# Layer 0's finish with gate and output matmuls as 64-row tiles, one column parity in each half of TensorE's array

## The chip, the cores and the metric

The kernel runs on one core of a Trainium2 chip. Its engines work side by side, each through its own instructions in order: TensorE (PE in the profile, and PEld for its weight loads) multiplies matrices into the accumulation memory PSUM, VectorE (DVE) and ScalarE (ACT) read PSUM and work elementwise, GpSimd (POOL) works elementwise on SBUF, SyncE (SP) issues the transfers. They wait for each other by semaphores. PSUM has 128 partitions and eight banks of 512 f32 columns. The metric is the device time of one execution in microseconds; lower is better.

## The reference

x is a 256 x 256 grid of tokens of 64 channels. Two layers follow each other, each added to x. What the change touches is the end of layer 0, the "finish": from the products p and from zn (the normalised input of the layer) it makes the output.

```python
p = jnp.einsum('bikc,bjkc->bijc', a, b)
x = _ln(p, ln_out_w, ln_out_b) @ w_z + b_z
g = jax.nn.sigmoid(zn @ w_g + b_g)
return x * g                       # and outside: x = x + this
```

## The kernel before

One partition row of the kernel's tiles holds two neighbouring tokens of 64 channels, an even and an odd column of the grid. So weights of 64 x 64 stand twice in a 128 x 128 matrix whose two other quarters are zero: `w_out` (in EFF) for the output and columns E_G to E_Z of `w_hi` and `w_lo` (EFF read as f16) for the gate. 128 partitions in, 128 columns out: partitions and columns 0 to 63 are the even tokens, 64 to 127 the odd ones.

Layer 0's finish goes over NG = 64 groups of GR = 4 grid rows, in 67 steps of a software pipeline that is written out by hand for each engine; nothing but these orders and the semaphores decides when something runs. In step s TensorE does, in this order:

- four transposes of the normalised p of group s (`pn` in WK, f32, line 752), when DVE and POOL have each written their half of it (pn_done, pn_done_p);
- the gate of group s (`project_gate`, line 486 through `mm`, tiles EFF and XT_ALL), for s >= AHEAD = 4: 12 matmuls of 128 x 128 in f16, three products for each of four rows. The gates of groups 0 to 3 are made ahead, at the end of the chunk loop. Gate g goes to PSUM bank g % 2, and waits until the sigmoid of group g-2 has read that bank (sg_done at g-1);
- the output z of group s-1 (line 486): the bias in one matmul of 512 columns (BROW, ONES), then four f32 matmuls of 128 x 128, each of which is two weight loads and two passes on the chip (EFF, WK). The transposed data `pt` is the stationary operand, w_out the moving one. z goes to bank 6 + (s-1) % 2 and waits until DVE has read group s-3 out of it (y_done);
- four transposes of the new x of group s-3 (f32, line 784).

ACT copies the transposed p to `pt` (line 964), takes the gate's sigmoid out of PSUM into `sg` (line 969), and splits off the high f16 part of the new x (line 977). DVE normalises half of pn (line 1420), multiplies z out of PSUM by sg, which is called y here (line 1429), makes the low f16 part of the new x (line 1443) and its statistics (line 1435). POOL normalises the other half of pn (line 1030) and adds y to x (line 1039). In DVE's steps 3, 6 and 9 a chain of four instructions (`rstd_rows`, lines 1365 to 1368) stands between pn and y; it makes the next quarter of the reciprocal deviations. Transfers of p and x run under all this.

In the chunk loop of both layers `project` already has units in two forms: with 128 rows, and, where `split_rows` says so, with 64-row matmuls whose two halves of the array work on the two column halves and write to two banks.

Of the kernel before, what the change touches and what calls it, by code (L numbers as in the profile page):

```python
# [34 lines left out]
CH = 64  # L35
P = 128
ROW = 2 * CH
GR = 4
# [13 lines left out]
AHEAD = 4  # L52
# [14 lines left out]
E_G = NQ * 2 * QW  # L67
# [21 lines left out]
def build(nc, x, mask, w0, w1, bias0, bias1, vecs, consts, norm_consts, spread, ones3, out):  # L89
# [4 lines left out]
    ALU = mybir.AluOpType  # L94
    ACT = mybir.ActivationFunctionType
# [10 lines left out]
    with ctx:  # L106
# [14 lines left out]
        BROW = sb("BROW", ROW, bf16)  # L121
        ONES3 = sb("ONES3", P, bf16)
# [7 lines left out]
        T = sb("T", 36)  # L130
        table_tmp = sb("table_tmp", 12)
        PS = ctx.enter_context(nc.psum_tensor("PS", [P, 8, BANK], f32))


        w_hi, w_lo = (EFF[:, 0:E_Z].bitcast(f16)[:, i * E_Z:(i + 1) * E_Z] for i in range(2))

        def half(g, i):

            return halves[:, ds(g * (2 * BANK) + i * BANK, BANK)]
# [71 lines left out]
        pt = WK[:, 6 * BANK:8 * BANK].rearrange("p (s n) -> p s n", s=2)  # L211
# [75 lines left out]
        g_done = sem("g_done")  # L287
        sg_done = sem("sg_done")
# [49 lines left out]
        def mask_tile(eng, n4, u):  # L338
# [2 lines left out]
            return eng.tensor_tensor(ab[:, :, :, ds(n4 * (4 * PR) + u * PR, PR)], sig[:, u],  # L341
                                     rows.unsqueeze(2).to_broadcast([P, 2, 2 * CHUNK, PR]), ALU.mult)

        def reached(eng, semaphore, value):

            if not isinstance(value, int) or value > 0:
                eng.wait_ge(semaphore, value)
# [136 lines left out]
        def _(pe):  # L484
            def mm(dst, lhsT, rhs, start=True, stop=True):
                return nc.tensor.matmul(dst, lhsT, rhs, start=start, stop=stop)  # L486
# [100 lines left out]
            for layer in range(2):  # L587
# [3 lines left out]
                def rows_times(bank, g, r, column):  # L591

                    dst = bank[:, r * ROW:(r + 1) * ROW]
                    hi, lo = (half(g, i)[:, r * P:(r + 1) * P] for i in range(2))
                    mm(dst, hi, w_hi[:, ds(column, ROW)], True, False)
                    mm(dst, hi, w_lo[:, ds(column, ROW)], False, False)
                    return mm(dst, lo, w_hi[:, ds(column, ROW)], False, True)
# [39 lines left out]
                        last.then_inc(proj_done[layer], 1)  # L637

                def project_gate(g):
                    if layer == 0:  # L640
                        for r in range(GR):
                            last = rows_times(PS[:, g if g < AHEAD else g % 2, :], g, r, E_G)
                        last.then_inc(g_done, 1)
                    else:
                        bank, hi, lo = PS[:, g % 4, :], w_hi[:, E_G:E_Z], w_lo[:, E_G:E_Z]
                        mm(bank, hi, half(g, 0), True, False)
                        mm(bank, lo, half(g, 0), False, False)
                        mm(bank, hi, half(g, 1), False, True).then_inc(gate1_done, 1)
# [96 lines left out]
                for step in range(NG + 3):  # L745
                    g = step
                    if g < NG:
                        pe.wait_ge(pn_done, g + 1)
                        pe.wait_ge(pn_done_p, g + 1)
                        reached(pe, pt_ready, g - 1)  # L750
                        for r in range(GR):
                            last = nc.tensor.transpose(PS[:, 4 + g % 2, r * P:(r + 1) * P], pn[:, g % 2, r, :], ident)  # L752
                        last.then_inc(tb_done, 1)
                    if AHEAD <= g < NG:

                        pe.wait_ge(sg_done, g - 1)
                        project_gate(g)
                    g = step - 1
                    if 0 <= g < NG:

                        pe.wait_ge(pt_ready, g + 1)
                        reached(pe, y_done, g - 1)
                        bank = PS[:, 6 + g % 2, :]
                        mm(bank, ONES3[:, :], BROW[:, :].unsqueeze(1).to_broadcast([P, GR, ROW]), True, False)
                        for r in range(GR):
                            last = mm(bank[:, r * P:(r + 1) * P], pt[:, g % 2, r * P:(r + 1) * P], w_out,
                                      False, r == GR - 1)
                        last.then_inc(z_done, 1)
                    g = step - 3
                    if 0 <= g < NG:  # L770

                        pe.wait_ge(xadd_done, g + 1)
                        if g < 2:

                            pe.wait_ge(sg_done, g + 3)
                        if g < NG - 2:

                            reached(pe, x1split_done, g - 1)
                        else:

                            pe.wait_ge(sg_done, NG)
                        for r in range(GR):
                            row = g * GR + r
                            last = nc.tensor.transpose(PS[:, new_x_bank(g), r * P:(r + 1) * P],  # L784
                                                       xb[:, row // HR % HS, row % HR, :], ident)
                        last.then_inc(x1tr_done, 1)
# [13 lines left out]
        def _(act):  # L800
# [55 lines left out]
            for layer in range(2):  # L856
# [99 lines left out]
                def finish_steps(g0, n_steps, lo):  # L956

                    for k in range(n_steps):
                        g = g0 + k
                        if lo[0] <= k < lo[1]:  # L960
                            act.wait_ge(tb_done, g + 1)

                            reached(act, z_done, g - 1)
                            nc.scalar.activation(pt[:, k % 2], PS[:, 4 + k % 2, :], ACT.Copy).then_inc(pt_ready, 1)
                            ahead = isinstance(g, int) and g < AHEAD
                            act.wait_ge(g_done, g + 1)

                            reached(act, xadd_done, g - 3)
                            nc.scalar.activation(sg[k % 4], PS[:, k if ahead else k % 2, :], ACT.Sigmoid,
                                                 scale=T[:, 22:23]).then_inc(sg_done, 1)  # L970
                        if lo[2] <= k < lo[3]:
                            h = g - 4

                            act.wait_ge(x1tr_done, h + 1)
                            act.wait_ge(bn_done, h + (1 + NG))
                            bank = new_x_bank(h) if isinstance(h, int) else 2 + k % 2
                            nc.scalar.activation(half(h, 0), PS[:, bank, :], ACT.Identity, scale=T[:, 25:26]
                                                 ).then_inc(x1t_ready, 1)
# [100 lines left out]
        def _(dve):  # L1079
# [228 lines left out]
            for layer in range(2):  # L1308
# [95 lines left out]
                def finish_steps(g0, n_steps, lo):  # L1404

                    for k in range(n_steps):
                        g = g0 + k
                        if lo[0] <= k < lo[1]:
                            s, u = (k // BG) % 2, k % BG
                            if u == 0:  # L1410

                                dve.wait_ge(p_in[s], g0 * 4 + 64)

                            reached(dve, tb_done, g - 1)

                            src = ptb[:, s].rearrange("p (c q) (r e) -> p q c r e", q=2, e=2)
                            dst = pn[:, k % 2].rearrange("p r (q c e) -> p q c r e", q=2, e=2)
                            tile = src[:, 0, :, u * GR:(u + 1) * GR, :]
                            rs = rstd2[:, 0, ds(g * GR, GR)].unsqueeze(1).unsqueeze(3)
                            ins = V.tensor_tensor(dst[:, 0], tile, rs.to_broadcast([P, CH // 2, GR, 2]), ALU.mult)  # L1420
                            ins.then_inc(pn_done, 1)
                            if isinstance(g0, int) and g0 == 0 and k in (3, 6, 9):
                                final(rstd_rows(k // 3), rstd_ready, k // 3)
                        if lo[2] <= k < lo[3]:
                            h = g - 2
                            dve.wait_ge(z_done, h + 1)
                            dve.wait_ge(sg_done, h + 1)
                            tile = sg[(k + 2) % 4]
                            V.tensor_tensor(tile, PS[:, 6 + k % 2, :], tile, ALU.mult).then_inc(y_done, 1)
                        split(k, g, lo)  # L1430
                        if lo[4] <= k < lo[5]:
                            h = g - 4
                            dve.wait_ge(x1tr_done, h + 1)
                            bank = new_x_bank(h) if isinstance(h, int) else 2 + k % 2
                            V.bn_stats(REC[:, ds(h * 6, 6)], PS[:, bank, :]).then_inc(bn_done, 1)
# [146 lines left out]
```

## Time and profile before

| what | us |
|---|---|
| median of three runs (lowest, highest) | 1107.92 (1107.46, 1108.34) |
| the profiled execution: its own time | 1107.85 |
| the profiled execution: span from first to last instruction | 1105.8 |
| TensorE busy, of the span | 997.5 (90%) |
| VectorE busy | 804.0 (73%) |
| ScalarE busy | 681.7 (62%) |
| GpSimd busy | 556.9 (50%) |

Busy times of an engine are summed over the whole program, whose stages have different limits. TensorE's matmuls overlap in its pipeline and their ends are modelled, so the distance from start to start says more of its pace than a busy share. The finish lies between 507 and 683 us of the span.

### The profile page before, as it was taken

What the parts mean: (1) busy time and instruction counts of PE and PEld (TensorE: products, weight loads), DVE (VectorE), ACT (ScalarE), POOL (GpSimd) and SP (SyncE); (2) the same over time, 40 slices, a digit from 0 to 9 for tenths busy, and PEclk for the clock granted to TensorE, in tenths of its full rate; (3) what the DMA queues carried; (4) which work ended last, traced back from release to release, by engine and by line L of the source; (5) the groups of instructions that cost most, each with busy time, mean ns of one, the idle gap of its engine ahead of it and who ended that gap; (6) DMA issues with size and microseconds to landing.
All of it is one profiled execution on the core that took longest, in us unless ns stands there. A gap on an engine that the chain in (4) does not pass through costs nothing.

```text
span 1105.8 us, 36355 instructions
## 1 busy us (share of the span) xinstructions
PE 997.5 (90%) x14204; PEld 780.1 (71%) x14204; DVE 804.0 (73%) x1270; ACT 681.7 (62%) x1102; POOL 556.9 (50%) x479
## 2 busy tenths in 40 slices
PE   5689798579999999996999997799999999789997
PEld 5543333248898888985999997587878787645554
DVE  6926988976786868767988888664646565567775
ACT  5747565365666656655676765484857667546665
POOL 0000644488092561904777774390937648146664
PEclk9989999869999999998999998799999999989999
DMA  9800000000301203069999760004031130599994
GB/s 349 317 9 1 0 1 0 1 2 4 134 24 78 78 22 134 4 181 231 226 208 203 180 149 1 2 4 154 5 104 54 46 111 4 167 196 285 294 276 153
DMA packets 173196, 121.32 MB, mean 110 GB/s; under 512 B 69764, under 2 KB 152068, under 8 KB 173064
## 3 DMA queue, kind: packets, MB, share of 16 engines
q1 hardware_dynamic: 173064, 119.34, 39.9%
q8 instruction: 110, 1.80, 0.7%
q14 instruction: 22, 0.18, 0.1%
HBM read 68.99 MB, written 50.33 MB: 108 GB/s over the span
## 4 chain that ended last, share of the span: by engine, by line
PE 77%; DVE 9%; DMA 4%; issue 4%; POOL 3%; ACT 2%; SPq 1%; DVEq 0%; POOLq 0%; ACTq 0%
PE PS L486 69%; DMA AB<-x 3%; PE PS L737 3%; PE PS L752 2%; PE PS L784 2%; DVE AB L1259 1%; POOL XT_ALL L994 1%; POOL AB L341 1%; DVE XT_ALL L1280 1%; DMA AB<-k_scratch 1%; PE PS L500 1%; DVE XT_ALL L1443 1%; ACT WK L874 1%; SPq L355 0%; DVE WK L1316 0%
## 5 line engine op out<-in xcount | busy, mean ns | idle before, releaser
L486 PE MATMUL PS<-EFF,XT_ALL 64*128 64x64 f16 (+1 forms) x10368 | 342.6, 201 | 8.7 <-POOL XT_ALL L994 3.6
L486 PEld LDWEIGHTS PS<-EFF,XT_ALL 64*128 64x128 f16 (+1 forms) x10368 | 315.5, 96 | 42.7 <-issue 16.9
L486 PE MATMUL PS<-AB 128*128 128x256 f16 (+3 forms) x1482 | 291.5, 348 | 36.3 <-ACT AB L841 10.6
L486 PEld LDWEIGHTS PS<-AB 128*128 128x128 f16 (+3 forms) x1482 | 200.9, 137 | 124.6 <-issue 34.0
L874 ACT ACTIVATE WK<-PS,T 128x512 f32<-128x512 f32 x256 | 174.7, 685 | 94.9 <-PE PS L486 82.8
L1059 POOL TENSOR_TENSOR AB<-WK,AB 128x512 f32 x128 | 144.8, 1162 | 111.8 <-ACT AB L884 110.8
L341 POOL TENSOR_TENSOR AB<-WK,MS 128x512 f32 x96 | 130.5, 1389 | 104.5 <-DVE WK L1316 104.5
L994 POOL TENSOR_TENSOR XT_ALL<-AB,XT_ALL 128x512 f32 (+1 forms) x59 | 69.8, 1192 | 166.5 <-DVE XT_ALL L1280 156.2
L1069 POOL TENSOR_TENSOR WK<-XT_ALL 128x512 f32 (+1 forms) x64 | 82.0, 1283 | 76.5 <-PE PS L737 51.1
L1324 DVE TENSOR_TENSOR WK<-PS,WK 128x512 f32<-128x512 f32 x128 | 85.8, 686 | 33.2 <-ACT WK L874 33.2
L1316 DVE TENSOR_TENSOR WK<-PS,WK 128x512 f32<-128x512 f32 x128 | 86.8, 688 | 30.1 <-ACT WK L874 23.4
L1340 DVE BATCH_NORM_STATS2 REC<-WK 128x512 f32 x64 | 44.4, 694 | 56.9 <-ACT WK L903 56.9
L925 ACT ACTIVATE WK<-PS,T 128x512 f32<-128x512 f32 x64 | 49.4, 777 | 51.5 <-PE PS L486 51.5
L836 ACT ACTIVATE XT_ALL<-PS,T,CF 128x512 f32<-128x512 f32 (+1 forms) x64 | 49.7, 776 | 49.6 <-PE PS L486 49.6
L903 ACT ACTIVATE WK<-PS,T 128x512 f32<-128x512 f32 x64 | 44.0, 687 | 51.8 <-PE PS L486 51.8
L910 ACT ACTIVATE WK<-PS 128x512 f32<-128x512 f32 x64 | 41.2, 644 | 47.0 <-PE PS L486 47.0
L486 PE MATMUL PS<-AB,EFF 128*128 128x512 f32 x128 | 67.5, 613 | 2.4 <-DMA AB<-k_scratch 2.4
L486 PEld LDWEIGHTS PS<-EFF,WK 128*128 128x128 f32 x512 | 68.1, 194 | 1.8
L486 PE MATMUL PS<-XT_ALL,AB 128*128 128x512 f32 (+1 forms) x128 | 68.8, 626 | 0.0
L1030 POOL TENSOR_TENSOR WK<-AB,S 128x256 f32<-128x256 f32 x64 | 50.7, 792 | 36.0 <-DVE S L1368 35.4
L486 PE MATMUL PS<-EFF,WK 128*128 128x128 f32 x512 | 68.3, 277 | 0.0
L1335 DVE TENSOR_TENSOR S<-S,WK 128x512 f32<-128x512 f32 x64 | 44.5, 695 | 31.9 <-ACT WK L910 30.9
(193 smaller groups left out, 1537.4 us busy)
## 6 DMA issues: line engine op xcount, KB each, us to landing
AB<-x SPq DMA_DIRECT2D x64, 512.0 KB, 7.0
p_scratch<-WK SPq DMA_DIRECT2D x32, 512.0 KB, 2.6
k_scratch<-WK SPq DMA_DIRECT2D x64, 256.0 KB, 2.1
AB<-k_scratch SPq DMA_DIRECT2D x32, 512.0 KB, 10.4
out<-AB SPq DMA_DIRECT2D x16, 1024.0 KB, 8.6
AB<-p_scratch SPq DMA_DIRECT2D x29, 512.0 KB, 7.6
AB<-p_scratch SPq DMA_DIRECT2D x2, 640.0 KB, 6.3
RAW<-w SPq DMA_DIRECT2D x2, 256.0 KB, 2.7
```

The source lines that it names most:

```text
L341: return eng.tensor_tensor(ab[:, :, :, ds(n4 * (4 * PR) + u * PR, PR)], sig[:, u], rows.unsqueeze(2).to_broadcast([P, 2, 2 * CHUNK, PR]), ...
L486: return nc.tensor.matmul(dst, lhsT, rhs, start=start, stop=stop)
L836: nc.scalar.activation(XT[:, ds(n * GR, GR), :].rearrange("p r n -> p (r n)"), PS[:, u % 4, :], ACT.Identity, bias=T[:, 15:16], scale=CF[: ...
L874: nc.scalar.activation(tile, unit(layer, u)[:, :, 0:2 * CHUNK, :], ACT.Sigmoid, scale=T[:, 22:23] if layer == 0 else T[:, 28:29]).then_inc ...
L925: nc.scalar.activation(gate1[:, k % 4], PS[:, k % 4, :], ACT.Sigmoid, bias=T[:, 32:33], scale=T[:, 28:29]).then_inc(gate1_ready, 1)
L994: nc.gpsimd.tensor_tensor(half(n, 1), zn[:, u % 8], half(n, 0), ALU.subtract).then_inc(lo_done, 1)
L1030: nc.gpsimd.tensor_tensor(dst[:, 1], src[:, 1, :, u * GR:(u + 1) * GR, :], rs.to_broadcast([P, CH // 2, GR, 2]), ALU.mult).then_inc(pn_don ...
L1059: nc.gpsimd.tensor_tensor(ab_rows(ab_lo, n8, u), sig1[:, u], ab_rows(ab_hi, n8, u), ALU.subtract).then_inc(ablo_done, 1)
L1069: nc.gpsimd.tensor_tensor(x1sum[:, k % 4], half(g, 0), half(g, 1), ALU.add).then_inc(x1sum_done, 1)
L1316: V.tensor_tensor(gate, lin, gate, ALU.mult).then_inc(prod_done[0], 1)
L1324: V.tensor_tensor(gate, lin, gate, ALU.mult).then_inc(prod_done[1], 1)
L1335: V.tensor_tensor(S1[:, :], S1[:, :], st[:, s, :, c % 2], ALU.add).then_inc(s1_done, 1)
```

## The change

For groups from AHEAD on, the gate is made by 64-row matmuls: for each of the 12 products one with partitions 0 to 63 and columns 0 to 63 into bank 0, and one with partitions 64 to 127 and columns 64 to 127 into bank 1. The zero quarters are no longer multiplied. Each bank holds 256 columns, so one group fills half of both banks, and all groups use the same two: the gate of group g waits for the sigmoid of group g-1. The output does the same with banks 6 and 7: two bias matmuls of 256 columns with all 128 rows, then for each row two f32 matmuls of 64 rows by 64 columns; z of group g waits for y of group g-1. The sigmoid and y read two banks through a rearranged access pattern; the elements and the results are as many as before.

```diff
+        def by_row(tile):
+            return tile.rearrange("p (r q c) -> p r q c", r=GR, q=2)
+        def by_parity(bank):
+            return PS[:, bank:bank + 2, 0:GR * CH].rearrange("p q (r c) -> p r q c", r=GR)
...
                 def project_gate(g):
-                    if layer == 0:
+                    if layer == 0 and g < AHEAD:
                         for r in range(GR):
-                            last = rows_times(PS[:, g if g < AHEAD else g % 2, :], g, r, E_G)
+                            last = rows_times(PS[:, g, :], g, r, E_G)
+                        last.then_inc(g_done, 1)
+                    elif layer == 0:
+                        for r in range(GR):
+                            hi, lo = (half(g, i)[:, r * P:(r + 1) * P] for i in range(2))
+                            for i, (x, w) in enumerate(((hi, w_hi), (hi, w_lo), (lo, w_hi))):
+                                for q in range(2):
+                                    rows = slice(q * CH, (q + 1) * CH)
+                                    last = mm(PS[:, q, r * CH:(r + 1) * CH], x[rows, :],
+                                              w[rows, E_G + q * CH:E_G + (q + 1) * CH], i == 0, i == 2)
                         last.then_inc(g_done, 1)
...
-                        pe.wait_ge(sg_done, g - 1)
+                        pe.wait_ge(sg_done, g)
...
-                        reached(pe, y_done, g - 1)
-                        bank = PS[:, 6 + g % 2, :]
-                        mm(bank, ONES3[:, :], BROW[:, :].unsqueeze(1).to_broadcast([P, GR, ROW]), True, False)
+                        reached(pe, y_done, g)
+                        for q in range(2):
+                            row = BROW[:, q * CH:(q + 1) * CH].unsqueeze(1).to_broadcast([P, GR, CH])
+                            mm(PS[:, 6 + q, 0:GR * CH], ONES3[:, :], row, True, False)
                         for r in range(GR):
-                            last = mm(bank[:, r * P:(r + 1) * P], pt[:, g % 2, r * P:(r + 1) * P], w_out,
-                                      False, r == GR - 1)
+                            for q in range(2):
+                                rows = slice(q * CH, (q + 1) * CH)
+                                last = mm(PS[:, 6 + q, r * CH:(r + 1) * CH], pt[rows, g % 2, r * P:(r + 1) * P],
+                                          w_out[rows, rows], False, r == GR - 1)
...
+                                nc.scalar.activation(by_row(sg[k % 4]), by_parity(0), ACT.Sigmoid,
+                                                     scale=T[:, 22:23]).then_inc(sg_done, 1)
...
-                            V.tensor_tensor(tile, PS[:, 6 + k % 2, :], tile, ALU.mult).then_inc(y_done, 1)
+                            V.tensor_tensor(by_row(tile), by_parity(6), by_row(tile), ALU.mult).then_inc(y_done, 1)
```

TensorE's program, one step of the finish once all parts run, before (752 the transposes of p, 784 those of x, 486 gate, bias and output; the last two numbers are partitions of the result by columns):

```order
L752 MATMUL PS<-CF,WK 128x128 [waits pt_ready,pn_done_p,pn_done]
L752 MATMUL PS<-CF,WK 128x128 x3
L486 MATMUL PS<-EFF,XT_ALL 128x128 [waits sg_done]
L486 MATMUL PS<-EFF,XT_ALL 128x128 x11
L486 MATMUL PS<-BROW,ONES 128x512 [waits y_done,pt_ready]
L486 MATMUL PS<-EFF,WK 128x128 x4
L784 MATMUL PS<-CF,AB 128x128 [waits x1split_done,xadd_done]
L784 MATMUL PS<-CF,AB 128x128 x3
```

Gate, bias and output follow each other there as 17 calls with 128 rows. The same step in the changed kernel, where the lines have moved to 769, 804 and 494:

```order
L769 MATMUL PS<-CF,WK 128x128 [waits pt_ready,pn_done_p,pn_done]
L769 MATMUL PS<-CF,WK 128x128 x3
L494 MATMUL PS<-EFF,XT_ALL 128x64 [waits sg_done]
L494 MATMUL PS<-EFF,XT_ALL 128x64 x23
L494 MATMUL PS<-BROW,ONES 128x256 [waits y_done,pt_ready]
L494 MATMUL PS<-BROW,ONES 128x256
L494 MATMUL PS<-EFF,WK 128x64 x8
L804 MATMUL PS<-CF,AB 128x128 [waits x1split_done,xadd_done]
L804 MATMUL PS<-CF,AB 128x128 x3
```

The gate has 24 matmuls of 64 columns for 12 of 128, the bias two for one, the output eight for four. The places of the waits in the row order are the same; their values are one group later.

TensorE's program at the start of the finish, the outputs of groups 0, 1 and 2, before:

```order
L486 MATMUL PS<-BROW,ONES 128x512 [waits pt_ready]
L486 MATMUL PS<-EFF,WK 128x128 x4
L752 MATMUL PS<-CF,WK 128x128 [waits pt_ready,pn_done_p,pn_done]
L752 MATMUL PS<-CF,WK 128x128 x3
L486 MATMUL PS<-BROW,ONES 128x512 [waits pt_ready]
L486 MATMUL PS<-EFF,WK 128x128 x4
L752 MATMUL PS<-CF,WK 128x128 [waits pt_ready,pn_done_p,pn_done]
L752 MATMUL PS<-CF,WK 128x128 x3
L486 MATMUL PS<-BROW,ONES 128x512 [waits y_done,pt_ready]
L486 MATMUL PS<-EFF,WK 128x128 x4
```

The first wait for y_done stands at the third output. The same place in the changed kernel, up to the output of group 1:

```order
L494 MATMUL PS<-BROW,ONES 128x256 [waits pt_ready]
L494 MATMUL PS<-BROW,ONES 128x256
L494 MATMUL PS<-EFF,WK 128x64 x8
L769 MATMUL PS<-CF,WK 128x128 [waits pt_ready,pn_done_p,pn_done]
L769 MATMUL PS<-CF,WK 128x128 x3
L494 MATMUL PS<-BROW,ONES 128x256 [waits y_done,pt_ready]
L494 MATMUL PS<-BROW,ONES 128x256
L494 MATMUL PS<-EFF,WK 128x64 x8
```

The wait for y_done has moved one output ahead, to that of group 1.

## Rows read from the trace of the kernel before

**Rows 1.** Busy time by engine in 20 us of the finish: us, engines, PEclk, DMA, GB/s.

```profile
540.00:560.00 20.00, 20.00 (x222) 19.73 (x221) 17.55 (x31) 13.79 (x23) 15.03 (x16) 1.00 1.04 219
```

**Rows 2.** Instructions in order of time, one steady step: start, us, engine, line, operation.

```profile
592.09 0.38 PE L486 MATMUL PS<-BROW,ONES 128*128 128x512 bf16 x1
592.29 0.69 ACT L969 ACTIVATE MS<-PS,T 128x512 f32<-128x512 f32 x1
592.31 1.05 PE L486 MATMUL PS<-EFF,WK 128*128 128x128 f32 x8
...
593.20 0.60 PE L784 MATMUL PS<-CF,AB 128*128 128x128 f32 x4
593.40 0.69 DVE L1429 TENSOR_TENSOR MS<-PS,MS 128x512 f32<-128x512 f32 x1 [0.32 <-PE PS L486]
...
593.64 0.60 PE L752 MATMUL PS<-CF,WK 128*128 128x128 f32 x4
...
594.07 0.83 PE L486 MATMUL PS<-EFF,XT_ALL 128*128 128x128 f16 x12
...
594.74 0.38 PE L486 MATMUL PS<-BROW,ONES 128*128 128x512 bf16 x1
```

**Rows 3.** Waits from 536 to 677 us: waiting, for whom, us, times, longest.

```profile
DVE MS L1429 <- PE PS L486: 8.4, 26, 0.3
```

**Rows 4.** The chain that ended last, from 500 to 705 us: start, us, what.

```profile
535.94 1.78 PE PS L486 x21
...
676.38 1.79 PE PS L486 x21
```

**Rows 5.** A 64-row and a 128-row unit of layer 0's projection: timeline and groups.

```profile
207.68 0.87 PE L486 MATMUL PS<-EFF,XT_ALL 64*128 64x64 f16 x48
...
L486 PE MATMUL PS<-EFF,XT_ALL 64*128 64x64 f16 x48 | 0.9, 190 | 0.0
...
208.48 1.34 PEld L486 LDWEIGHTS PS<-EFF,XT_ALL 128*128 128x128 f16 x24
```

**Rows 6.** Weight loads begun as a 64-row and a 128-row unit starts: us, PEld busy.

```profile
207.67:207.70 0.03, 0.02 (x4) 1.00 0.00 0
...
208.47:208.51 0.04, 0.03 (x2) 1.00 0.00 0
```

**Rows 7.** f32 weight loads outside the finish, in order of time.

```profile
85.43 0.30 PEld L486 LDWEIGHTS PS<-CF,AB 128*128 128x128 f32 x2
85.54 0.28 PE L486 MATMUL PS<-CF,AB 128*128 128x1 f32 x2
85.65 0.30 PEld L486 LDWEIGHTS PS<-XT_ALL,AB 128*128 128x128 f32 x2
...
694.46 0.49 PEld L486 LDWEIGHTS PS<-RAW,EFF 64*128 64x128 f32 x2 [2.95 <-DVE EFF L1474]
...
697.29 0.50 PEld L486 LDWEIGHTS PS<-AB,CF 128*128 128x128 f32 x2 [1.19 <-DVE AB L1134]
```

**Rows 8.** f32 matmuls that change between 128 and 2 rows, in order of time.

```profile
75.28 0.39 PE L486 MATMUL PS<-RAW,AB 128*128 128x128 f32 x2
...
75.60 0.48 PE L486 MATMUL PS<-AB,CF 2*128 2x128 f32 x2
76.01 0.30 PEld L486 LDWEIGHTS PS<-VEC,RAW 128*128 128x128 f32 x2
```

**Rows 9.** The first reciprocal chain of the finish, in order of time.

```profile
514.48 0.38 PE L486 MATMUL PS<-BROW,ONES 128*128 128x512 bf16 x1
...
515.69 0.69 DVE L1429 TENSOR_TENSOR WK<-PS,WK 128x512 f32<-128x512 f32 x1
...
516.77 0.66 PE L752 MATMUL PS<-CF,WK 128*128 128x128 f32 x4 [0.58 <-DVE WK L1420]
```

**Rows 10.** The end of the finish, in order of time.

```profile
678.20 0.69 DVE L1429 TENSOR_TENSOR MS<-PS,MS 128x512 f32<-128x512 f32 x1 [0.69 <-PE PS L486]
...
678.43 0.38 PE L486 MATMUL PS<-BROW,ONES 128*128 128x512 bf16 x1
```

More of the change, by code:

```diff
@@ L968, in finish_steps @@
                             reached(act, xadd_done, g - 3)
-                            nc.scalar.activation(sg[k % 4], PS[:, k if ahead else k % 2, :], ACT.Sigmoid,
-                                                 scale=T[:, 22:23]).then_inc(sg_done, 1)
+                            if ahead:
+                                nc.scalar.activation(sg[k % 4], PS[:, k, :], ACT.Sigmoid,
+                                                     scale=T[:, 22:23]).then_inc(sg_done, 1)
+                            else:
+                                nc.scalar.activation(by_row(sg[k % 4]), by_parity(0), ACT.Sigmoid,
+                                                     scale=T[:, 22:23]).then_inc(sg_done, 1)
                         if lo[2] <= k < lo[3]:
```

## The prediction

> **What bounds the kernel now.** I read the table of busy time by stretch first, to see which engine is full in the finish: in a 20 us piece of it TensorE is busy all the time at a granted clock of 1.00 (2.4 GHz), DVE 17.55 us [rows 1]. Then the timeline of one step, for what TensorE does in it and how fast: from one bias to the next, 592.09 to 594.74, a step takes 2.65 us, and each piece begins where the one before it ends [rows 2]. The waits of this stretch have DVE waiting for TensorE before y (26 times in one of its two forms, 0.3 us at most) and no row with TensorE as the one that waits [rows 3]. The chain that ended last runs through the same TensorE pieces from 535.94 to 676.38, which is 53 steps of 2.65 us [rows 4]. So what the change does to TensorE's step counts in full there, as long as the step stays above DVE's work in it: 17.55 us in 20, so 2.33 us a step.
>
> **The parts of a step before**, from start to start [rows 2]: bias 0.22; output eight passes in 0.89, so 0.111 each; transposes of x 0.44 and of p 0.43, so 0.11 each; gate 12 in 0.67, so 0.056 each. Sum 2.65.
>
> **Gate.** Pairs of 64-row matmuls exist in layer 0's projection. 48 of them take 0.87 us to the end of the last, which is recorded as 0.19 long, so 24 pairs start within 0.68: 0.029 a pair [rows 5]. 24 matmuls of 128 rows take there what they take in the finish (24 loads in 1.34). The gate becomes 12 x 0.029 = 0.35, 0.32 less. The bias keeps its columns, two times 256 for 512: no change but one more short load that lies under the first pass.
>
> **Output.** Here the question is what sets the 0.111 of a pass: its moving columns, which halve, or its weight load, which doesn't. An f32 load shows alone where the matmul has a single column: the loads at 85.43 (two) and 85.65 are 0.22 apart in two, so 0.11 each, though there is next to nothing to stream [rows 7]. So the load already sets the pace, and here the stationary side is pt with 128 columns, before and after. Do 64 rows load faster than 128? At half the clock two loads of 64 rows take 0.49 and two of 128 rows 0.50 [rows 7]: no. The Trainium skill has the same in its page "TensorE: Matmul & The Clock Gate", section "LDWEIGHTS (loading the stationary operand)": the time goes with the columns of the stationary operand and not with its rows. By its formula 128 columns would take an estimated 107 ns, and the trace's f32 loads agree; it speaks against this half of the change.
>
> The eight passes become sixteen with a load each. What remains is whether the loads of the two halves run side by side. At the start of a 64-row unit four loads begin within 0.03 us, two for each half; at the start of a 128-row unit two within 0.04 [rows 6]. The second half's load doesn't wait for the first half's, so I take them as side by side. In program order a row has both passes of the first half, then both of the second. The first half's second pass waits 0.11 for its load, the second half's first pass follows it at once, its second pass 0.11 later. So a row takes 0.225 and four rows, to the end of the last pass (0.055), 0.96 instead of 0.89: 0.07 more. The bounds: were a pair set by its columns alone, 8 x 0.055 = 0.45; were all 16 loads one after another, 16 x 0.111 less the first (which is counted below) plus 0.055 = 1.72. I take 0.96, by the loads' rows.
>
> **Changes of form.** A step now goes 128 rows (transposes), 64 (gate), 128 (bias), 64 (output), 128: four changes where it had none. The last of the 64-row matmuls in [rows 5] starts at 207.68 + 0.87 - 0.19 = 208.36, and the 128-row unit's first load only at 208.48, 0.09 later than the pace would have it. In f32 a pair of 128 rows starts at 75.28 and would be through 0.22 later, at 75.50; the 2-row form's first load stands at 75.60, and the next change comes at 76.01, 0.41 on: two passes (0.22), one bare load (0.11), and again 0.09 of nothing [rows 8]. So a change costs 0.10, both ways, and the load behind it is bare: 0.01 in f16 and bf16, 0.11 in f32. The gate's start and the bias's start cost 0.11 each, the output's start and the transposes' start 0.20 each: 0.62. No wait of another engine covers this, since TensorE is the one that is waited for. The Trainium skill states the cause in "TensorEngine Tiling (Array Packing)", section "Key Properties": changing the tiling mode drains the engine. The trace agrees, with 0.10.
>
> **The step after:** 2.65 - 0.32 + 0.07 + 0.62 = 3.02 us, 0.37 more. 53 steps: 19.6 us.
>
> **The new waits.** In the steady steps they are free. The gate of a group must wait for the sigmoid before it: that starts at 592.29 and takes 0.69, and the next gate starts at 594.07 [rows 2]. z must wait for the y before it: 593.40 + 0.69 = 594.09, the next bias at 594.74 [rows 2], 0.65 to spare; between the last output pass and the next bias lie two sets of transposes, the gate and three changes, over 1.5 us after the change too. ACT's sigmoid and DVE's y read as many elements as before and stay.
>
> At the start they are not free. In step 3 y of group 1 stands on DVE behind the first reciprocal chain and starts at 515.69; z of group 2 started at 514.48, during the chain [rows 9]. It must now wait until 516.38. The first two outputs run at half the clock and push all that by about 0.5. From 516.9 z takes 0.22 + 0.20 + 0.96, then come the change and transposes of x (0.20 + 0.44), and the transposes of p start at 518.9 instead of 516.77 [rows 9]: 2.1 later. Behind them wait gate and z of that step. At the chains of steps 6 and 9 DVE is late anyway and the wait mostly lies under it; four steps between cost 0.37 each, 1.5. Together 3.6, between 1.5 and 6. At the end z of group 63 starts at 678.43, and y of group 62 runs from 678.20 for 0.69 [rows 10]: the wait and the longer output cost about 1.0 in all.
>
> **Sum:** 19.6 + 3.6 + 1.0 = 24.2 us. The profiled execution took 1107.85 (span 1105.8 and 2.05 around it), which is 0.07 below the median of the runs shown, so no correction: 1107.85 + 24.2 = 1132.
>
> **Rivals.** (1) Faster: the halves really halve the output, 0.45 instead of 0.96. The step is 2.51, 0.14 less, 53 of them 7.4, less perhaps 1 us lost at the start: 1101. For it speaks that the f16 pairs halve [rows 5], against it the bare loads of [rows 7]. It decides if an f32 load of 64 rows takes less than about 0.07 us in a running stream, where the step comes out even. The skill's tiling page holds this out in its section "Theoretical Speedup": up to 2 times where the contracted or the moving dimension is 64 or less. By that rule the output would cost 0.45 and the time would be that of this rival; the page gives no trace for f32, and no run here shows it. (2) Slower by much: f32 loads of the two halves share one path and go one after another. The output is 1.72, the step 3.78, 53 x 1.13 = 60, the start 6: 1174. For it speaks only that all rows on loads in pairs are f16, whose loads are short enough to hide an order. (3) No change: the drain costs less here than in the projection, because the transposes of x need no result of the output. The step is even if the four changes and bare loads cost 0.25 instead of 0.62; nothing in [rows 8] speaks for it. Time 1108.
>
> **How the numbers follow.** The mechanism above has 0.79, rival 1 0.09, rival 2 0.08, rival 3 0.04. The likeliest one's own range is 1124 to 1142: steps of 0.30 to 0.45 more (16 to 24 us) with the start between 1.5 and 6 and the end. For 8 in 10 I stretch it to 1116 below and 1150 above, for loads that overlap a little better or worse than in two equal halves; rivals 1 and 2 lie outside. About 0.2% (2 us) is what a measurement of this kernel tells from no change. Faster 0.09, same 0.04, slower 0.87.
>
> **What would show it.** In the profile after: a step from bias to bias of 3.0 us, TensorE still the chain; the gate's 24 matmuls within 0.35 to 0.4; the two weight loads of different halves of the output beginning within a few ns and each 0.11 from the next of its half; 0.1 of nothing at each of four places, and a bare load before the first output pass and the first transpose; DVE waiting longer before y; TensorE waiting for DVE at the first chain. Wrong, if the output's 16 passes take about 0.5 or 1.7 instead of 0.96; if the gaps at the changes are missing; if TensorE waits for the sigmoid or for y in every step; or if the granted clock of the finish falls under the 1.00 it has now.

## The result, and the profile after

The changed kernel takes 1124.14 us (median of four runs, 1122.74 to 1124.86) beside 1108.13 us of the kernel before on the same chip (1107.46 to 1108.82): a ratio of 1.0143, 95% interval 1.0125 to 1.0160. It is slower, by 16 us; the forecast said 24 us, with 1116 to 1150 as its range. The profiled execution spans 1121.9 us, 16.1 more than before.

Where these 16.1 us lie is read from the chain that ended last, 500 to 720 us (start, us, what):

```profile
508.36 1.94 PE PS L769 x8
...
541.84 1.82 PE PS L494 x42
...
692.48 1.84 PE PS L494 x42
700.16 1.89 DVE T L1138
```

The two pieces at 541.84 and 692.48 answer to those of [rows 4] (42 instructions in place of 21: gate 24, bias 2, output 16): 53 steps lie between them, in 150.64 us instead of 140.44, so 2.842 us a step instead of 2.65. That is 10.2 us. From the first transposes, 508.36, to the first of these pieces it takes 33.48 us; before, 508.19 to 535.94, 27.75. That is 5.7 us more at the start. From the last of them to DVE's statistics behind the finish it takes 7.68 instead of 7.18, 0.5 more, and the rest of the program 0.3 less.

One steady step in order of time (start, us, engine, line, operation; PEld are the weight loads), which answers to [rows 2]:

```profile
592.40 0.60 PE L769 MATMUL PS<-CF,WK 128*128 128x128 f32 x4
...
592.94 0.53 PE L494 MATMUL PS<-EFF,XT_ALL 64*128 64x64 f16 x24
...
593.39 0.39 PE L494 MATMUL PS<-BROW,ONES 128*128 128x256 bf16 x2
593.53 0.68 ACT L993 ACTIVATE WK<-PS,T 128x512 f32<-128x512 f32 x1
593.71 0.97 PEld L494 LDWEIGHTS PS<-EFF,WK 64*128 64x128 f32 x16 [0.21 <-issue]
593.72 1.11 PE L494 MATMUL PS<-EFF,WK 64*128 64x64 f32 x16
...
594.75 0.66 PE L804 MATMUL PS<-CF,AB 128*128 128x128 f32 x4
594.87 0.69 DVE L1453 TENSOR_TENSOR MS<-PS,MS 128x512 f32<-128x512 f32 x1 [0.52 <-PE PS L494]
595.14 0.47 PEld L769 LDWEIGHTS PS<-CF,WK 128*128 128x128 f32 x4
595.25 0.60 PE L769 MATMUL PS<-CF,WK 128*128 128x128 f32 x4
```

From start to start: transposes of p 0.54 (before 0.43), gate 0.45 (0.67), bias 0.33 (0.22), output 1.03 (0.89), transposes of x 0.50 (0.44). The gate with the change behind it is 0.22 shorter, everything else is longer. The 16 loads of the output take 0.97 to the end of the last, of which each takes 0.19 (187 ns is the mean of their group from 590 to 600 us): so the last pair begins 0.78 behind the first, which is seven distances of 0.111. That the two halves load side by side shows where the first two begin (loads in a stretch: us, PEld busy):

```profile
593.70:593.73 0.03, 0.02 (x2) 1.00 0.38 102
```

The waits of the finish, 536 to 690 us (waiting, for whom, us, times, longest), beside [rows 3]:

```profile
PEld PS L494 <- issue: 20.5, 108, 0.2
DVE MS L1453 <- PE PS L494: 13.5, 26, 0.5
...
PE PS L494 <- DVE MS L1453: 0.8, 1, 0.8
```

DVE waits 0.5 before y where it waited 0.3, and TensorE itself waits once in the whole stretch, at 539.40, behind the third reciprocal chain: in the steady steps the later values of the two waits cost nothing. The first row is the weight loads' idle time with no releaser, at two places in each step: 0.17 ahead of the gate and 0.21 ahead of the output, two of the four places where the form changes.

### The profile page after: what moved, and what is told of

Read it like the earlier page. It is cut to its first block, busy times and chain, and to the rows that moved or that the text cites. A ratio compares the mean times of both kernels' runs of the same rounds, so it can differ in the third digit from the quotient of the medians.

```text
span 1121.9 us, 38943 instructions
## 1 busy us (share of the span) xinstructions
PE 1012.9 (90%) x15495; PEld 767.8 (68%) x15500; DVE 826.6 (74%) x1270; ACT 675.0 (60%) x1102; POOL 548.4 (49%) x479
## 4 chain that ended last, share of the span: by engine, by line
PE 67%; DVE 12%; issue 9%; DMA 4%; POOL 3%; ACT 2%; DVEq 1%; SPq 1%; POOLq 0%; ACTq 0%; another core or an unknown queue 0%
PE PS L494 61%; DVE WK L1416 4%; PE PS L804 3%; DMA AB<-x 3%; PE PS L769 3%; DVE AB L1283 1%; POOL XT_ALL L1018 1%; POOL AB L341 1%; DVE XT_ALL L1304 1%; DMA AB<-k_scratch 1%; PE PS L508 1%; DVE WK L1420 1%; ACT WK L894 1%; SPq L363 0%; DVE WK L1340 0%
## 5 line engine op out<-in xcount | busy, mean ns | idle before, releaser
L494 PE MATMUL PS<-EFF,XT_ALL 64*128 64x64 f16 (+1 forms) x11088 | 324.8, 198 | 8.7 <-POOL XT_ALL L1018 3.6
L494 PEld LDWEIGHTS PS<-EFF,XT_ALL 64*128 64x128 f16 (+1 forms) x11088 | 295.4, 96 | 52.2 <-issue 26.8
L1093 POOL TENSOR_TENSOR WK<-XT_ALL 128x512 f32 (+1 forms) x64 | 73.8, 1155 | 83.9 <-PE PS L754 58.4
L984 ACT ACTIVATE WK<-PS 128x512 f32<-128x512 f32 x64 | 38.2, 597 | 75.5 <-PE PS L769 75.5
L1420 DVE SCALAR_TENSOR_TENSOR WK<-WK,T 128x512 f32<-128x512 f32 x64 | 76.1, 1189 | 6.7
L494 PEld LDWEIGHTS PS<-EFF,WK 64*128 64x128 f32 x1024 | 65.4, 196 | 14.3 <-issue 14.3
L494 PE MATMUL PS<-EFF,WK 64*128 64x64 f32 x1024 | 74.4, 287 | 0.0
L930 ACT ACTIVATE WK<-PS 128x512 f32<-128x512 f32 x64 | 41.2, 643 | 47.0 <-PE PS L494 47.0
```

What stands on the lines that cost most here:

```text
L1093: nc.gpsimd.tensor_tensor(x1sum[:, k % 4], half(g, 0), half(g, 1), ALU.add).then_inc(x1sum_done, 1)
L1420: V.scalar_tensor_tensor(x1sum[:, k % 4], x1sum[:, k % 4], col(24), gate1[:, k % 4], ALU.mult, ALU.add).then_inc(o_done, 1)
```

## The experiments

The stretch from the first transposes of p to the bias of the tenth output (group 9), read from TensorE's timeline, measures the start below: 28.25 us before (508.19 to 536.44), 33.87 after (508.36 to 542.23).

**The waits alone.** All matmuls have the old form, but the gate has one bank and the output has one, with the changed kernel's waits.

```diff
-                            last = rows_times(PS[:, g if g < AHEAD else g % 2, :], g, r, E_G)
+                            last = rows_times(PS[:, g if g < AHEAD else 0, :], g, r, E_G)
...
-                        pe.wait_ge(sg_done, g - 1)
+                        pe.wait_ge(sg_done, g)
...
-                        reached(pe, y_done, g - 1)
-                        bank = PS[:, 6 + g % 2, :]
+                        reached(pe, y_done, g)
+                        bank = PS[:, 6, :]
...
```

> The kernel before with the single buffering alone: gate and output keep their 128-row form, each on one bank, and wait for the sigmoid and for y of the group just before. Theory A (the 0.19 us that each steady step gained are the form changes of TensorE's array; the new waits cost only at the start of the finish): the steady step stays 2.65 us, only the start gets longer, by 3 to 6 us, so 1111 to 1114. Rival B (the new waits cost in every step): a step near 2.84 and 1120 to 1124.

Measured: 1109.43 us beside 1108.23, ratio 1.0012 (1.0002 to 1.0021). The step is as before, from one bias to the next in TensorE's timeline:

```profile
598.53 0.38 PE L486 MATMUL PS<-BROW,ONES 128*128 128x512 bf16 x1
...
601.18 0.38 PE L486 MATMUL PS<-BROW,ONES 128*128 128x512 bf16 x1
```

2.65 us. The start takes 29.13, 0.9 more. The output of group 2 does wait for y there:

```profile
516.78 0.38 PE L486 MATMUL PS<-BROW,ONES 128*128 128x512 bf16 x1 [1.05 <-DVE WK L1429]
```

It begins 8.33 us after the first transpose, 2.0 later than before the change (514.48 - 508.19 = 6.29). But most of that doesn't last. From 508 us until the tenth output TensorE waits 2.8 us for y in this run, and before the change it waited 2.3 us for DVE at other places of the same steps, ahead of transposes: DVE with its chains is late there either way. So the single buffers cost about 1 us in all, and not the 3.6 that the forecast had for them; most of the changed kernel's 5.7 at the start must have another cause.

**The gate alone** in 64-row matmuls with its wait, bias and output as before:

```diff
-                        reached(pe, y_done, g)
-                        for q in range(2):
-                            row = BROW[:, q * CH:(q + 1) * CH].unsqueeze(1).to_broadcast([P, GR, CH])
-                            mm(PS[:, 6 + q, 0:GR * CH], ONES3[:, :], row, True, False)
+                        reached(pe, y_done, g - 1)
+                        bank = PS[:, 6 + g % 2, :]
+                        mm(bank, ONES3[:, :], BROW[:, :].unsqueeze(1).to_broadcast([P, GR, ROW]), True, False)
...
```

> Only the gate as 64-row matmuls on half of two banks, single buffered; the output as in the kernel before. Theory A: the gate from its first load to the bias takes 0.46 instead of 0.67 and the change of form before it costs 0.09, so a step of 2.53 us, 53 x 0.12 = 6.3 us less, and no lost time at the start since z has its old wait: about 1102. Rival B (waits): the wait for the sigmoid shows in every step, 1108 or more.

Measured: 1102.71 us beside 1108.23, ratio 0.9954 (0.9937 to 0.9971). TensorE's timeline:

```profile
595.29 0.39 PE L494 MATMUL PS<-BROW,ONES 128*128 128x512 bf16 x1
...
597.38 0.53 PE L494 MATMUL PS<-EFF,XT_ALL 64*128 64x64 f16 x24
597.83 0.39 PE L494 MATMUL PS<-BROW,ONES 128*128 128x512 bf16 x1
```

A step of 2.54 us, 0.11 less: 0.32 won by the halves, and two changes of form of 0.10 each paid. The gate's half of the change is a gain.

**The output alone**, the gate as before (gate and sigmoid with two banks, waits one group back):

```diff
-                    elif layer == 0:
...
-                                    last = mm(PS[:, q, r * CH:(r + 1) * CH], x[rows, :],
-                                              w[rows, E_G + q * CH:E_G + (q + 1) * CH], i == 0, i == 2)
...
+                            last = rows_times(PS[:, g if g < AHEAD else g % 2, :], g, r, E_G)
...
```

> Only the output as 64-row matmuls on half of two banks, single buffered, with its two bias matmuls; the gate as in the kernel before. Theory A: bias, output and the transposes of x gain 0.31 us a step (two form changes of 0.1, bare loads, nothing saved in the output's passes): a step of 2.96, 53 x 0.31 = 16.4, and the start's 5.5: about 1130, slower than the whole change. Rival C (64-row passes make the output itself faster, and it is the gate's form that costs): under 1120.

Measured: 1129.60 us, ratio 1.0204 (1.0187 to 1.0222). TensorE's timeline:

```profile
595.38 0.38 PE L494 MATMUL PS<-BROW,ONES 128*128 128x256 bf16 x2
595.69 1.11 PE L494 MATMUL PS<-EFF,WK 64*128 64x64 f32 x16
596.73 0.66 PE L795 MATMUL PS<-CF,AB 128*128 128x128 f32 x4
...
598.33 0.38 PE L494 MATMUL PS<-BROW,ONES 128*128 128x256 bf16 x2
```

A step of 2.95 us, 0.30 more. With the gate's 0.11 less the sum is 0.19 more, which is the changed kernel's step: the two halves of the change add up, and the output's half is the whole loss. Its start takes 32.6 us, so most of the start's loss is the output's too.

**Two changes of form fewer.** The bias is put ahead of the gate, so that gate and output, both in 64-row matmuls, follow each other:

```diff
-                    if AHEAD <= g < NG:
-
-                        pe.wait_ge(sg_done, g)
-                        project_gate(g)
                     g = step - 1
...
                             mm(PS[:, 6 + q, 0:GR * CH], ONES3[:, :], row, True, False)
+                    g = step
+                    if AHEAD <= g < NG:
+
+                        pe.wait_ge(sg_done, g)
+                        project_gate(g)
```

> The changed kernel with one thing moved: in each step the two bias matmuls stand ahead of the gate, so that gate and output follow each other in the 64-row form: two form changes a step instead of four, and the output's first load lies under the gate. The same matmuls, the same bytes. Theory A: 0.09 and 0.10 for the two changes and 0.05 for the bare load fall away: a step of 2.60 us, 53 x 0.24 = 12.8 us less than the changed kernel, about 1111. Rival B (waits): the bias waits for y earlier than before, so no faster than the changed kernel, 1124 or more.

Measured: 1115.05 us, ratio 1.0065 (1.0048 to 1.0082). TensorE's timeline:

```profile
595.14 0.65 PE L807 MATMUL PS<-CF,AB 128*128 128x128 f32 x4
...
596.40 0.52 PE L494 MATMUL PS<-EFF,XT_ALL 64*128 64x64 f16 x24
596.76 1.08 PE L494 MATMUL PS<-EFF,WK 64*128 64x64 f32 x16
597.78 0.66 PE L807 MATMUL PS<-CF,AB 128*128 128x128 f32 x4
```

A step of 2.64 us where the changed kernel has 2.84: two changes fewer save 0.20, so 0.10 each. The expected 2.60 was too low, since I had the output's first load hidden behind the gate; the output still takes 1.02, as its loads only begin when the gate's 24 are through.

**Half the moving columns.** The output passes have 32 columns instead of 64; the second half of each parity's output channels is left out.

```diff
-                                last = mm(PS[:, 6 + q, r * CH:(r + 1) * CH], pt[rows, g % 2, r * P:(r + 1) * P],
-                                          w_out[rows, rows], False, r == GR - 1)
+                                last = mm(PS[:, 6 + q, r * CH:r * CH + CH // 2], pt[rows, g % 2, r * P:(r + 1) * P],
+                                          w_out[rows, q * CH:q * CH + CH // 2], False, r == GR - 1)
```

> The changed kernel with 32 moving columns instead of 64 in each output matmul; the second half of the output channels of each parity is left out. The number of passes and of weight loads stays. Theory A (the output is paced by its f32 weight loads, 0.11 us for each pair): the steady step stays 2.84 us. Rival C (it is paced by its columns): eight pairs by 0.027 less, a step of 2.63.

Measured, in a single run: 1133.29 us beside 1108.41. TensorE's timeline:

```profile
600.62 0.66 PE L804 MATMUL PS<-CF,AB 128*128 128x128 f32 x4
...
602.43 1.08 PE L494 MATMUL PS<-EFF,WK 64*128 64x32 f32 x16
603.44 0.66 PE L804 MATMUL PS<-CF,AB 128*128 128x128 f32 x4
```

The output takes 1.01 instead of 1.03, the step 2.82 instead of 2.84. Half the columns are worth 0.02 us: the loads set the pace of these passes. The time is 9 us longer than the changed kernel's all the same, and that lies at the start (windows: us, engines, PEclk, DMA, GB/s):

```profile
530.00:540.00 10.00, 10.00 (x101) 8.22 (x100) 4.69 (x9) 3.73 (x6) 4.09 (x5) 0.50 0.39 105
...
550.00:560.00 10.00, 10.00 (x180) 8.15 (x178) 7.41 (x14) 5.85 (x10) 6.51 (x7) 0.93 0.41 107
```

The granted clock is 0.50 (1.2 GHz) until 551 us, while TensorE is recorded busy all the time.

**The bias in 64-row matmuls too**, so that gate, bias and output have one form. Its three parts are laid out once, ahead of layer 0, so that each half's rows hold those of its parity:

```diff
-                            row = BROW[:, q * CH:(q + 1) * CH].unsqueeze(1).to_broadcast([P, GR, CH])
-                            mm(PS[:, 6 + q, 0:GR * CH], ONES3[:, :], row, True, False)
+                            rows = slice(q * CH, (q + 1) * CH)
+                            row = BROW[rows, rows].unsqueeze(1).to_broadcast([CH, GR, CH])
+                            mm(PS[:, 6 + q, 0:GR * CH], ONES3[rows, :], row, True, False)
...
```

> The changed kernel with the bias of the output in the 64-row form too: its three bf16 parts stand in rows 0 to 2 and again in rows 64 to 66, and each half of the array makes the bias of its parity. A step has then one stretch of 128 rows (transposes) and one of 64 rows (gate, bias, output). Theory A: two form changes less (0.20, as the run with the bias ahead of the gate showed) and the two bias matmuls side by side (0.11 less): a step of 2.53 us; 53 x 0.31 = 16.4 us less than the changed kernel, the longer start stays: about 1108. Rival: the changes cost only where a load of another type follows, then 2.73 and 1118.

Measured: 1101.50 us beside 1108.41, ratio 0.9936 (0.9920 to 0.9953): faster than the kernel before. TensorE's timeline:

```profile
599.78 0.66 PE L805 MATMUL PS<-CF,AB 128*128 128x128 f32 x4
...
600.80 0.53 PE L494 MATMUL PS<-EFF,XT_ALL 64*128 64x64 f16 x24
601.16 0.27 PE L494 MATMUL PS<-BROW,ONES 64*128 64x256 bf16 x2
601.27 1.00 PE L494 MATMUL PS<-EFF,WK 64*128 64x64 f32 x16
602.21 0.66 PE L805 MATMUL PS<-CF,AB 128*128 128x128 f32 x4
```

A step of 2.43 us (2.45 on average over the 53, as a few are longer). Against the changed kernel the gate saves 0.09 (no change behind it), the bias 0.22 (no change, and its two halves run side by side: 0.11), the output 0.09, because its first loads now begin with the bias, at 601.16. I had expected 2.53, without this last term and with the bias at its old length. DVE has little left to wait now: 19.32 us of 20 are its own work between 540 and 560, so TensorE's step could hardly become shorter with effect.

**The old form at the start.** The outputs of groups 0 to 13 have the old form, banks and wait; all others, and the gates, are the changed kernel's.

```diff
-                        reached(pe, y_done, g)
...
+                        if g < 14:
+                            reached(pe, y_done, g - 1)
+                            bank = PS[:, 6 + g % 2, :]
...
+                                last = mm(bank[:, r * P:(r + 1) * P], pt[:, g % 2, r * P:(r + 1) * P], w_out,
+                                          False, r == GR - 1)
+                        else:
+                            reached(pe, y_done, g)
...
```

> The changed kernel, but the outputs of groups 0 to 13 in the 128-row form on alternating banks, as before the change. Theory D (the 5.6 us lost at the start come from the outputs in their new form there: they keep TensorE at the granted clock of 0.5 until 527 us instead of 513): the clock rises at 512 to 514 us, the tenth output starts 28.2 us after the first transpose of the finish as before the change, later steps take 2.84; with the first steps also shorter, about 1117. Rival E (the single-buffered gate, or chance, keeps the clock down): 1122 to 1124.

Measured: 1117.99 us, ratio 1.0089 (1.0073 to 1.0106), 6.2 us less than the changed kernel. The start takes 28.0 us again and the later steps 2.84. What the clock does is seen in windows; first the changed kernel's:

```profile
516.00:520.00 4.00, 4.00 (x27) 3.18 (x26) 1.46 (x4) 1.18 (x2) 1.95 (x2) 0.50 1.34 217
...
524.00:528.00 4.00, 4.00 (x48) 3.25 (x49) 3.30 (x6) 1.28 (x3) 2.02 (x2) 0.60 1.20 295
528.00:532.00 4.00, 4.00 (x67) 3.43 (x66) 3.62 (x8) 2.44 (x4) 2.02 (x2) 1.00 0.54 130
```

then the kernel before:

```profile
512.00:516.00 4.00, 4.00 (x32) 3.87 (x31) 3.46 (x7) 2.35 (x4) 1.95 (x2) 0.89 1.26 234
```

and the one with the old start:

```profile
512.00:516.00 4.00, 4.00 (x25) 3.81 (x24) 2.99 (x6) 1.51 (x4) 1.94 (x2) 0.67 1.30 248
516.00:520.00 4.00, 4.00 (x55) 3.57 (x55) 3.54 (x7) 2.74 (x5) 3.04 (x3) 1.00 1.35 218
```

In the changed kernel the clock rises at 527.2 (0.60 in 524 to 528 is 0.8 us at 1.00 and the rest at 0.50), with the old start at 514.6, before the change at 512.8. The later waits alone do not keep it down, since in the first experiment it also rose at 514.6, nor does the gate alone (513.3). So with the outputs in their new form TensorE stays at 1.2 GHz for some 13 us longer. Other executions agree: the granted clock averaged over the whole span is 0.954 to 0.956 in the changed kernel's four, and 0.956 to 0.959 in the four with the old start. What it costs stands in the changed kernel's timeline:

```profile
516.20 0.69 DVE L1453 TENSOR_TENSOR WK<-PS,WK 128x512 f32<-128x512 f32 x1 [0.19 <-PE PS L494]
...
517.04 0.58 PE L494 MATMUL PS<-BROW,ONES 128*128 128x256 bf16 x2
...
522.11 0.60 PE L494 MATMUL PS<-BROW,ONES 128*128 128x256 bf16 x2
...
522.65 1.97 PE L494 MATMUL PS<-EFF,WK 64*128 64x64 f32 x16
...
527.21 0.39 PE L494 MATMUL PS<-BROW,ONES 128*128 128x256 bf16 x2
...
527.53 1.11 PE L494 MATMUL PS<-EFF,WK 64*128 64x64 f32 x16
```

Two steps of 5.07 and 5.10 us, which take 2.84 at full clock: 4.5 us more, beside the 5.7 that the start lost. They are not simply a part of the 5.7: before the change the first of these two steps took 3.45 us at full clock (bias at 514.48 and 517.93), because it met DVE's first chain.

**Gates in pairs.** With the output as before, two groups' gates are made in every second step, each in its half of the two banks; so the two changes around the gate come every second step.

```diff
-                    if AHEAD <= g < NG:
+                    if AHEAD <= g < NG and g % 2 == 0:
...
                         project_gate(g)
+                        project_gate(g + 1)
...
```

> The gate alone in the 64-row form, output as before the change, and the gates of two groups made together in every second step, each on its half of the columns of banks 0 and 1. The same matmuls as the run with the gate alone, half as many form changes. Theory A: 0.18 us less in every second step, so steps of 2.45 us on average instead of 2.54, 53 x 0.09 = 4.8 us less: about 1098. Rival B (the burst makes the sigmoid or the gate wait): no faster than the gate alone, 1102.7.

Measured: 1102.63 us, ratio 0.9947 (0.9931 to 0.9964): no better than the gate alone with 1102.71. The waits, 545 to 670 us:

```profile
PEld PS L769 <- DVE WK L1442: 5.9, 25, 0.2
```

In every second step TensorE now waits 0.24 for DVE's half of the normalised p. The long and the short step together take 5.10 us (bias at 600.03 and at 605.13), so 2.55 each, as with the gate alone: the change saved is waited for instead, because DVE is late after the short step (2.00 us from bias to bias, where DVE's work in a step is 2.3). The time is the rival's, but neither the gate nor the sigmoid is what is waited for.

**The two gains together.** Bias, gate and output in one form, and the old form for the outputs of groups 0 to 13:

```diff
+                        if g < 14:
+                            reached(pe, y_done, g - 1)
...
+                        else:
+                            reached(pe, y_done, g)
                             for q in range(2):
                                 rows = slice(q * CH, (q + 1) * CH)
...
+                                row = BROW[rows, rows].unsqueeze(1).to_broadcast([CH, GR, CH])
+                                mm(PS[:, 6 + q, 0:GR * CH], ONES3[rows, :], row, True, False)
...
```

> Two of the earlier runs joined: bias, gate and output in the 64-row form in one stretch of each step (two form changes), but the outputs of groups 0 to 13 in the 128-row form on alternating banks. Theory A with D: the start as in the run with the old start (the fifteenth output 40.7 us after the first transpose, the clock up at about 514 us), then steps of 2.43 to 2.45 as in the run with the 64-row bias: 2.6 to 3 us less than that run, about 1098.5, under both kernels of the change. Rival: what the old start saves comes back at the end of the finish, then 1101.5.

Measured: 1097.63 us (1096.53 to 1099.74) beside 1109.28, ratio 0.9906 (0.9889 to 0.9922). The start takes 28.0, the later steps 2.43. It beats the kernel before by 10 us by the ratio, 12 by the medians, and the changed one by 26. The gate alone already had 5 of that; the output's tiles, with the bias in their form and the old start, add as much again. Two windows, start and steady:

```profile
512.00:516.00 4.00, 4.00 (x32) 3.80 (x31) 3.45 (x7) 2.35 (x4) 1.94 (x2) 0.91 1.32 236
...
560.00:580.00 20.00, 20.00 (x408) 18.11 (x406) 19.27 (x34) 14.13 (x25) 16.29 (x17) 1.00 0.97 215
```

The clock rises as early as before (512.7), and DVE is nearly as full as TensorE: 19.27 us of 20.

## Why the prediction was right or wrong

**Gate, 0.32 less: right.** The gate alone shortens the step by 0.11 with two changes of 0.10 in it.

**Changes of form, 0.10 each: right.** With two fewer the step loses 0.20. Two of them leave 0.11 of the gate's 0.32; the output, which wins nothing, pays for two with nothing against them. It is the form that counts and not the type: f16 gate, bf16 bias and f32 output follow each other without the 0.10 once all have 64 rows (sixth experiment). The Trainium skill's sentence in "TensorEngine Tiling (Array Packing)", section "Key Properties", that a new mode drains the engine, agrees; the runs show the lost time, not the draining itself.

**Output, load-bound: right in its mechanism, too large in its size.** That 32 columns instead of 64 change the output by 0.02 us rules out rival 1. The rule of the Trainium skill's page "TensorEngine Tiling (Array Packing)" behind that rival, up to twice as fast where one dimension is 64 or less (section "Theoretical Speedup"), holds here for the f16 gate (0.67 to 0.35 us without its change) and not for the f32 output. That the halves load side by side rules out rival 2: it forecast 3.78 us a step. But the step's sum was 3.02 and the measured one is 2.84. The failing terms are two. The 0.96 of the output's passes let the second half run one load behind the first, so that eight distances of 0.11 lie between the first load and the last; the loads show seven, 0.78 us. From the output's first load to that of the transposes it takes 1.04, where the forecast's terms give 0.11 + 0.96 + 0.10 = 1.17. And the transposes' bare f32 load was put at 0.11, as for a matmul; the transposes of x take 0.50 instead of 0.44, so it costs 0.06. Together 0.13 + 0.05 = 0.18 a step, so that 53 steps cost 10.2 us and not 19.6.

**The waits.** Free in the steady steps: right. At the start the sum had 3.6 us for z of group 2 waiting for y behind the first reciprocal chain [rows 9] and for the steps behind it. That step fell. In the old form the wait and its 2.0 us do appear (first experiment), but they are not kept: TensorE had been waiting for DVE in these steps before the change too, and 0.9 is left at the tenth output. In the changed kernel hardly any wait is left to see: y of group 1 ends at 516.89 and z of group 2 follows at 517.04, but the weight loads have been idle for only 0.27 us there, because TensorE itself comes late; its one recorded wait for y is the 0.76 at 539.40. The start cost 5.7 all the same, by something that the forecast had as a small addition ("the first two outputs run at half the clock"): four outputs run wholly at half the clock (1.97 us for their 16 passes in the timeline, 1.11 for the fifth), since the clock rises at 527.2 and not at 512.8 as before the change. That 5.7 lies within the 1.5 to 6 given for the start is luck. The end's 1.0 measured 0.5.

**Rival 3**, no change because the changes of form are cheap, fell with the fourth experiment: they cost 0.10 each.

So the sum of 24.2 had 9.4 too much in the step and 0.5 at the end, and 2.1 too little at the start; with the 0.3 that the rest of the program gave back this is the measured 16.1. The two errors partly cancelled, which is luck. That the start's loss comes from the outputs' form is shown by undoing it there, their bias and banks with it; why that form leaves the clock low is not shown.

## What to carry to other kernels

Before splitting matmuls into row tiles, count the changes of form in one turn of the loop and price them from the trace, here 0.10 us each: tiles pay when neighbouring work takes the same form, as the bias in the sixth experiment, which turned 1.4% slower into 0.6% faster. Halving the moving columns of the f32 matmuls gained nothing here, where the stationary operand kept its 128 columns, because the loads set the pace. And a new form has to be looked at where the clock is low as well: read the granted clock in the first steps of a stage, and keep the old form there if it brings the clock up earlier.

## What the runs showed of the hardware that was not expected

TensorE's clock rose late wherever the finish began with the f32 outputs in 64-row form. In the changed kernel the granted clock stayed at 0.50 (1.2 GHz) until 527 us, in the other kernels that start the finish with these outputs until 523 to 530, with 32 moving columns until 551; with the old form there it rose to 1.00 between 512.7 and 514.6. The Trainium skill says in "TensorE: Matmul & The Clock Gate", section "What's actually happening", that the clock follows how busy the engine has been lately. Recorded busy time does not show that here: from 512 to 524 us TensorE was recorded busy for all of each 4 us in the changed kernel, and the clock stayed low. The ends of matmuls are modelled, so pauses may hide in this busy time; the weight loads were idle for 0.41 us ahead of each of the four outputs at half the clock. What in this form keeps the clock low is not shown by any run here, and stays open.

The f32 load ahead of transposes is bare for 0.06 us after a change of form, where the forecast had 0.11 from f32 matmuls [rows 7].
